# Two graph layers over eight batches: three tiles a batch in rounded halves, 1/z moved, the first batch reordered

## The reference

```python
# x: (8, 2048, 128), adj: (8, 2048, 2048), float32
h = x @ W;  f1 = h @ a1;  f2 = h @ a2
e = f1 + swapaxes(f2, 1, 2);  e = where(e >= 0, e, 0.2 * e)
attention = softmax(adj * e, axis=1)
x1 = attention @ h + bias + x
support = x1 @ W1 + b1
y = adj @ support
y = relu((y - mean(y)) * rsqrt(var(y) + 1e-5) * gamma + beta)   # mean, var over batches and nodes
out = y + x1
```

## Time and profile before

| | |
|---|---|
| three timed runs, us | 942.08, 943.45, 945.23; median 943.45 |
| the profiled execution, us | 945.52 |
| its span, us | 943.7, 9327 instructions |
| busy: PE, PEld | 885.1 (94%), 557.4 (59%) |
| busy: ACT, DVE, POOL | 800.3 (85%), 715.6 (76%), 293.2 (31%) |
| DMA | 238.03 MB, mean 252 GB/s |
| mean granted clock of PE | 0.967 of 2.4 GHz |

### The profile page before, as it was taken

One profiled execution on the slowest core, in us unless ns is written; L12 is line 12 of the kernel. 1 busy time (PEld: TensorE's weight loads), 2 busy tenths in 40 slices (PEclk: granted clock), 3 DMA queues, 4 the chain that ended last, 5 costly groups with the idle time before them and its releaser, 6 DMA issues.

```text
span 943.7 us, 9327 instructions
## 1 busy us (share of the span) xinstructions
PE 885.1 (94%) x3167; PEld 557.4 (59%) x3167; DVE 715.6 (76%) x789; ACT 800.3 (85%) x619; POOL 293.2 (31%) x390
## 2 busy tenths in 40 slices
PE   7898999999999999999999999999999999999970
PEld 5333656675566756666566756667566666666850
DVE  1654677798678877798778977788777886789966
ACT  4897779997899979998899969999799987997745
POOL 0112241254223442272422641252521633235000
PEclk8999999999999999999999999999999999999995
DMA  8986474867567584766658574765757666565968
GB/s 320 422 342 224 167 274 169 309 224 268 196 241 266 178 321 170 272 248 223 265 217 296 201 307 158 261 242 196 306 189 274 248 224 230 184 232 184 421 285 334
DMA packets 48527, 238.03 MB, mean 252 GB/s; under 512 B 5816, under 2 KB 6440, under 8 KB 23904
## 3 DMA queue, kind: packets, MB, share of 16 engines
q1 hardware_dynamic: 48480, 237.44, 67.4%
HBM read 213.18 MB, written 24.23 MB: 252 GB/s over the span
## 4 chain that ended last, share of the span: by engine, by line
PE 79%; POOL 5%; DMA 4%; DVE 4%; issue 4%; ACT 1%; SPq 1%; DVEq 0%; ACTq 0%; POOLq 0%
PE acc L512 34%; PE acc L481 11%; PE acc L483 11%; PE acc L487 10%; PE acc L469 4%; DMA adj_slot<-adjT 3%; PE acc L493 3%; PE acc L446 3%; DVE scores L728 2%; POOL hz_lo L881 2%; POOL hz L866 2%; POOL hz_hi L878 2%; PE acc L525 1%; PE acc L528 1%; PE acc L527 1%
## 5 line engine op out<-in xcount | busy, mean ns | idle before, releaser
L749 DVE TENSOR_TENSOR exp_lo<-scores,hi 128x2048 fp32r<-128x2048 f32 (+1 forms) x133 | 273.9, 2072 | 123.7 <-ACT hi L622 123.4
L728 DVE CUSTOM_DVE_ANT_0 scores<-scores,adj_slot 128x2048 f32<-128x2048 f32 x128 | 298.8, 2334 | 50.2 <-ACT scores L601 21.6
L608 ACT ACTIVATE scores<-scores,neg_mx 128x2048 f32<-128x2048 f32 x128 | 255.8, 1998 | 26.9 <-DVE neg_mx L731 26.9
L622 ACT CAST hi<-scores 128x2048 fp32r<-128x2048 f32 (+1 forms) x133 | 214.9, 1631 | 63.1 <-PE acc L487 59.0
L601 ACT ACTIVATE scores<-adj_slot,f_cols 128x2048 f32<-128x2048 f32 x128 | 255.8, 2004 | 9.8 <-issue 5.2
L512 PE MATMUL acc<-adj_slot,region_even 128*128 128x512 f32 x512 | 228.7, 592 | 0.0
L512 PE MATMUL acc<-adj_slot,region_odd 128*128 128x512 f32 x392 | 175.3, 592 | 0.8 <-DVE region_odd L782 0.8
L481 PE MATMUL acc<-hi,hz_lo 128*128 128x512 f32 x448 | 161.1, 482 | 13.6 <-POOL hz_lo L881 13.6
L512 PEld LDWEIGHTS acc<-adj_slot,region_even 128*128 128x128 f32 x512 | 96.8, 190 | 100.0 <-issue 95.8
L481 PEld LDWEIGHTS acc<-hi,hz_lo 128*128 128x128 f32 x448 | 85.0, 191 | 73.8 <-issue 43.5
L483 PE MATMUL acc<-hi,hz_hi 128*128 128x512 f32 x448 | 124.8, 402 | 0.0
(11 more groups left out here) (76 smaller groups left out, 600.9 us busy)
## 6 DMA issues: line engine op xcount, KB each, us to landing
adj_slot<-adjT SPq DMA_DIRECT2D x151, 1024.0 KB, 4.9
adj_slot<-xT SPq DMA_DIRECT2D x12, 1024.0 KB, 9.8
adj_slot<-biasT SPq DMA_DIRECT2D x32, 256.0 KB, 6.4
xp_dram<-adj_slot SPq DMA_DIRECT2D x32, 256.0 KB, 2.5
adj_slot<-xp_dram SPq DMA_DIRECT2D x8, 1024.0 KB, 9.0
adj_slot<-f_rows SPq DMA_DIRECT2D x7, 1024.0 KB, 7.1
adj_slot<-y_dram SPq DMA_DIRECT2D x7, 1024.0 KB, 9.2
outT<-adj_slot SPq DMA_DIRECT2D x6, 1024.0 KB, 5.5
```

The source lines that it names most:

```text
L608: act.activation(scores[e][:, :], scores[e][:, :], ACT.Exp, bias=neg_mx[:, e:e + 1], accum_out=zsum[:, e:e + 1]).then_inc(exp_done, 1)
L622: act.copy(hi[m][:, part_cols(t, i)], scores[e][:, part_cols(t, i)]).then_inc(hi_done, 1)
L728: dve.tensor_tensor_reduce(scores[e][:, :], scores[e][:, :], slots[s][:, :], 1.0, NEG_BIG, ALU.mult, ALU.max, mx[:, e:e + 1]).then_inc(max ...
L749: dve.tensor_tensor(exp_lo[e][:, part_cols(t, i)], scores[e][:, part_cols(t, i)], hi[m][:, part_cols(t, i)].bitcast(F32), ALU.subtract).th ...
```

## The change

Three tiles of layer 1 in each of the seven overlapped batches (k = 6, 9 and 12) are done by `layer1_halves`, in twelve float32r matmuls rather than four of float32. The tile's rounded half comes from memory by a DMA that casts, issued on POOL, into a slot that is free just then: slot 10 for k = 6, and slots 3 and 4, whose new tile DVE has already read, for k = 9 and 12 (`HI_AT`, `LENT`). SP loads what was in the lent slots again. DVE subtracts (`tile_low`), and POOL splits the support (`split_support`).

1/z no longer scales h. ACT rounds the exponentials times 1/z, DVE's subtraction multiplies by 1/z too, and POOL splits h itself in blocks of 256 columns (`split_h`). So `exp_high` waits for `recip`; `edge(t + 2)` now stands before it, and `exp_low` runs one tile later. The residual gets slot 11 (`T_RES`), in one piece, and all its sums come at the end of a batch. In the first batch the loads of x, w1, b1, gamma and beta stand further back, and DVE instead of ACT copies h and the f rows out of PSUM.

```diff
+    HI_AT = {6: T_X, 9: 3, 12: 4}
+    LENT = {HI_AT[k]: k for k in HI_AT if HI_AT[k] not in (T_BIAS, T_X)}
-    F_STEP = {1: 0, 2: 0, 3: 1, 4: 3, 5: 5, 6: 7, 7: 8}
+    X_AFTER = {1: 1, 2: 3, 3: 4, 4: 5, 5: 7, 6: 8, 7: 9}
+    F_STEP = {1: 1, 2: 2, 3: 3, 4: 4, 5: 6, 6: 7, 7: 9}
...
-                        if k == 3:
+                        if k == 6:
                             load_again(pv, T_X)
+                        for t in LENT:
+                            if LENT[t] == k:
+                                load_again(bt, t)
...
-                        if k == 7:
-                            load_residual(bt, 0)
...
+                        if k == 4:
+                            load_again(pv, T_RES)
+                        if k == T_RES + 2:
+                            load_residual(bt)
...
+            def layer1_halves(bt, k):
+                t = SIGMA[k]
+                tile_hi = slots_lo[HI_AT[k]]
+                pe.wait_ge(part_lo_done, split_no(bt, k))
+                pe.wait_ge(hi_loaded[k], 16 * (bt.n + 1))
+                for c in range(NC):
+                    pe.matmul(acc1[c][:, :], part_lo[bt.par][:, tile_cols(t)], tile_hi[:, cols(c)], start=False, stop=False)
+                for c in range(NC):
+                    pe.matmul(acc1[c][:, :], part_hi[:, :], tile_hi[:, cols(c)], start=False, stop=False)
+                pe.wait_ge(tile_lo_done, split_no(bt, k))
+                for c in range(NC):
+                    mm = pe.matmul(acc1[c][:, :], part_hi[:, :], slots_lo[l1_slot(bt, t)][:, cols(c)],
+                                   start=False, stop=False)
...
             def exp_high(bt, t):
...
-                act.wait_ge(exp_done, NT * bt.n + t + 1)
+                act.wait_ge(rz_done, NT * bt.n + t + 1)
...
-                    act.copy(hi[m][:, part_cols(t, i)], scores[e][:, part_cols(t, i)]).then_inc(hi_done, 1)
+                    act.activation(hi[m][:, part_cols(t, i)], scores[e][:, part_cols(t, i)], ACT.Copy,
+                                   scale=rz[:, e:e + 1]).then_inc(hi_done, 1)
...
+            def tile_low(bt, k):
...
+                dve.wait_ge(hi_loaded[k], 16 * (bt.n + 1))
+                dve.tensor_tensor(slots_lo[l1_slot(bt, t)][:, :], slots[l1_slot(bt, t)][:, :],
+                                  slots_lo[HI_AT[k]][:, :].bitcast(F32), ALU.subtract).then_inc(tile_lo_done, 1)
...
-                    if not is_first(bt):
+                    if not is_first(bt) and 1 < t < NT - 1:
+                        exp_low(bt, t - 1)
+                    if not is_first(bt) and (t == 0 or t >= NT - 2):
                         exp_low(bt, t)
+                    for k in HI_AT:
+                        if not is_first(bt) and max(k - 3, 0) == t:
+                            tile_low(bt.prev(), k)
...
+            def load_hi(bt, k):
...
+                    pool.wait_ge(max_done, NT * nx.n + HI_AT[k] + 1)
...
+                pool.dma_start(slots_lo[HI_AT[k]][:, :], adjT[bt.n, tile_cols(SIGMA[k]), :]).then_inc(hi_loaded[k], 16)
```

260 lines of the change are left out of this document (165 added, 95 removed).

## The result

| | before | changed |
|---|---|---|
| median of the timed runs, us | 944.34 (942.08 to 946.03, 4 runs) | 918.49 (915.42 to 921.88, 4 runs) |
| ratio | | 0.973, 95% interval 0.969 to 0.977 |
| span of the profiled execution, us | 943.7 | 916.1 |
| first batch, us | 97.88 | 87.52 |
| the seven overlapped batches, us | 765.97 | 749.38 |

A forecast was written before the change was run, and what follows sets the result against it. PE was taken to set the pace, with ACT 0.37 us behind. Halves 14.4, batch-start wait 2.2, clock 6.5 and first batch 11 sum to 34.1 us, from 943.45 to 909.3; range 895 to 928.

The forecast's parts named there:

- Halves in layer 1: Layer 1 on PE: 21 tiles fall from 3.43 to 2.74 us, 0.69 saved each, 14.4 us in all.
- Transfers: Six MB more a batch: one late load early in layer 0 costs 1.1 us, between bounds of nothing and 2.5.
- the upper bound (2.5): Transfers after a batch's start: one MB more ahead of the critical load, 2.5 us a batch.
- step 3: Place in a batch where DVE's first added subtraction, 2.29 us, falls, with little cover.
- 1/z in the exponentials' halves: Batch start: POOL's operations on h no longer need 1/z; ACT's rounding does, +0.10 us each; the 1.92 us wait goes.
- The clock: PE's clock after batch starts: falls cost 9.7 us in six batches; two thirds, 6.5 us, come back.
- The first batch: Adjacency tile 1 loads third, not sixth; layer 0 starts at 22.8, batch ends at 86.5 instead of 98.04; 11 us taken.
- B: Rival, chance 0.22: extra MB make tiles of steps 4 to 6 late by 2 us, clock falls as before; 918.
- D: Rival, chance 0.10: ACT and DVE become the bound, ACT's rounding waiting behind DVE's subtraction, 0.3 us a step; about 929.
- E: Rival, chance 0.06: casting loads land late, 18 to 23 us after issue eating the gain; at 25 us, about 975.

The follow-up runs named there:

- the run with one gap: Changed kernel, but PE waits for the low part ahead of all twelve products of layer 0's second tile, not only the last four: 924.93 us.
- the run with two tiles: Changed kernel with only k = 9 and 12 in halves and their casting loads issued 6 and 12 us later: 906.53 us, ratio 0.959.

## Why the prediction came out as it did

909.3 was forecast, 918.5 measured, in the range (895 to 928) and faster, as said. Of the 9.2 us between them 6.5 are in the spans (34.1 forecast, 27.6 measured); the other 2.7 lie in the profiled run of before, 2.1 above the median the forecast took, and that of the change, 0.6 below its own. That the total came into the range is in part luck: halves with their loads came out 12.2 us worse than forecast, and 1/z with the clock 5.5 better. By its own steps, in spans:

- **Halves in layer 1.** The size on PE is right: 0.72 a tile for 0.69. The step that failed is the one on *Transfers*, the term of 1.1 us a batch for one late load. Alone, five of the six MB cost 17.2 / 7 = 2.5 us a batch (with the first casting load at a somewhat earlier place), the size of the upper bound (2.5) that the prediction had worked out and not taken. It looked at one load in one place; three tiles in a batch come late (3, 4 and 5), DVE and PE are late by them at the second tile, the fourth and the last. And it put the subtraction in step 3, "where there is little cover", without a price: it meets the late load ahead of the same score. Forecast for halves and loads together was 14.4 - 7.7 = 6.7 us of gain. They lose 5.5. The **sign of this part was wrong**, and it was hidden in a total that came out faster.
- **1/z in the exponentials' halves.** Without halves the seven batches fall from 765.97 to 743.9 (like for like), 22.1 us. The forecast was 13.6 of wait, less 3.5 for POOL and DVE blocking one another, and 6.5 of clock: 16.6. It was better than that: PE's waits on low parts are 0.7 in all, and the clock came back whole. ACT's pointer operand is 2.00 us for the cast's 1.90 as taken, and DVE's subtraction 2.33.
- **The clock.** All six falls are gone, 9.7 us in place of the 6.5 taken. The reason given (shorter waits, spread over several tiles) fits the run with one gap, where five falls came back in the profiled execution.
- **The first batch.** 10.4 of 11, by other terms than given. Layer 0 starts at 22.35 (22.8 forecast) and `make_h` of batch 1 at 87.5 (87). But it was to start at the end of PE's `make_h`, and that ended at 19.96; it waited 2.39 us for h times 1/z, which POOL began at 21.85, and that wait was followed by a fall of the clock. Tile 1 landed at 13.8, not at 16.6: four small loads, costed at nothing, were 2.8 us of its delay before. The place of the three loads of x, the reason that the forecast gave, is worth 3.0 of the 10.4; the shares of the small loads, the residual's own slot and the copies on DVE were not separated.
- **The rivals.** B had 918, and the number is right with half of its mechanism: the start stayed dear, by late MB, but the clock did not fall. D's mechanism (DVE's subtraction of an adjacency tile ahead of the score, ACT's rounding behind it) is there, but at one place a batch, the fourth tile; without halves ACT's step fits and PE never waits. E did not: casting loads land after 9.2 us (median), not 18, and DVE never waits for one. The Trainium skill, "SBUF — State Buffer", section "SBUF: two separate sides", would have DMAs issued from GpSimd starve beside DVE instructions in a two-port mode. The load issued at 324.44, inside DVE's subtraction of 324.09 to 326.42, landed 10.0 us later, and those of the run with two tiles after 5.9; no starving shows in either. Ahead of the one of 324.44 two loads of SP were still under way, issued at 321.14 and 321.51 and landed at 327.66 and 331.41, so it fits queueing; whether these DVE instructions are in such a mode no row shows.

What was forecast to be seen: layer 0 at about 23, batches of 105 to 107 (106.3 to 108.1), clock 0.98 or more, PE waiting for DVE's low parts. The batches were the one sign that was missed, by up to 1.1 us, and of the signs of being wrong neither DVE's wait for the casting DMA nor ACT's for `rz` in mid-batch came.

## What to carry to other kernels

A step that trades the bound engine's time for MB must be priced at the first engine that waits for loads, not at the mean DMA share: here 0.65 busy seemed to leave room, and five MB a batch cost 2.5 us. Where an operation is added to an engine, look whether its place already holds a wait on something that the same change makes late; moving two issues and three subtractions a batch by one or more steps was worth 8 us over seven batches, with the same work. And take a bundle apart even when its total is a gain: one of these three parts lost.
